# Pairing the value products of two key tiles in an interleaved attention kernel

## The chip, the cores and the metric

One core of one Trainium2 chip runs the kernel. The metric is the device time of one execution in microseconds, lower is better. Engines: TensorE (PE: matmuls; PEld: its weight loads), VectorE (DVE), ScalarE (ACT), GpSimd (POOL) and the DMA queues, which SyncE (SP) mostly issues.

## The reference

A pre-norm transformer layer in float32 on 2 sequences of 1024 tokens, width 512. The attention has 32 query heads of 16 and one key/value head for all of them, with ALiBi slopes and a causal mask:

```python
qkv = layernorm(x) @ Wqkv                      # 32 heads of q, one k, one v, each 16 wide
scores = einsum('bqhd,bkd->bhqk', q, k) * 16 ** -0.5 + alibi, causal
x = x + (softmax(scores) @ v) @ Wo
y = layernorm(x)
x = x + y @ W_base.T + b_base + lora_of_the_top_2_of_8_experts(y)
```

## The kernel before

The kernel has three stages: projections (to about 160 us of the profile), attention (to about 625 us), and the output projection with the feed-forward part. The change lies in the attention.

**Units and steps.** A unit is 4 heads of one sequence on 512 queries. Two units make a step's work: "early" (queries 0 to 511, 4 key tiles of 128) and "late" (queries 512 to 1023, 8 key tiles). So a unit pair has NTI = 12 tiles, numbered 0 to 11: 0 to 3 early, 4 to 11 late. A tile on the diagonal needs only part of the queries: tiles 0 to 3 are 512, 384, 256 and 128 queries wide, tiles 4 to 8 are 512 wide, and 9, 10, 11 are 384, 256 and 128 wide. There are NK = 16 unit pairs, and PE's step k (0 to 17) computes the row maxima of pair k among the scores and values of pair k - 1.

**Three kinds of PE work** are interleaved in a step; one instruction stream issues them in order.

- A *slot*, m0 to m41 (`max_slot`, line 561): bf16 matmuls into one of NSB = 3 PSUM banks (0 to 2). VectorE then takes the row maximum of it (line 972 for full slots, line 967 for diagonal ones). A slot waits until VectorE has freed the slot three before it (`slot_free`, line 543). Slots m0, m1, m17, m18 are 2 heads of 128 keys, m2, m3, m23, m24 are 2 heads of 256, m4 to m7 and m29 to m32 are 384 keys of one head, and the rest 512 keys of one head, but for m15 and m41: these transpose the finished maxima (line 550), for which VectorE must have finished the slots before them.
- A *score piece*, written S4.0, S4.1 and so on for tile and half (`scores`, lines 585 and 588): two heads at 2 banks, or all four heads for the narrow tiles 2, 3, 10 and 11, which have one piece. There are 2 score buffers, so a piece waits until ScalarE's exponential of the piece two before it has finished (`exp_done`, line 578). ScalarE (`exps`, line 791) writes the exponentials to `probs[:, n % 4]`, four tiles deep, and on diagonal tiles GpSimd zeroes the future (line 1152).
- A *value product*, V0 to V11 (`values_product`, line 606): for each of 4 heads a float32 matmul with a 128x32 weight into 32 of the 128 partitions of bank 7. Each matmul becomes two instructions, so a tile has 8. It waits for the tile's exponentials and its zeroing, and, at tiles 0 and 4, for ScalarE's copy of bank 7 (`copy_unit`, line 803) of the unit before.

`pe_order(k)` writes the order. Value products lag the scores by LAG = 2 tiles, so V10 and V11 of the pair before (marked ') fall into the next step. The slots are spread over the pieces by the columns of work done so far, each piece's own included, so that a large piece is preceded by many slots. For steps 2 to 15 it gives:

```
m0 S0.0 m1 m2 V10' m3 S0.1 m4 S1.0 V11' m5 S1.1 m6 m7 S2.0 m8 m9 V0 m10 S3.0 m11 m12 V1
m13 S4.0 m14 V2 m15 S4.1 m16 m17 S5.0 V3 m18 m19 S5.1 m20 S6.0 m21 m22 V4 m23 m24 S6.1 m25 S7.0
m26 m27 m28 V5 m29 S7.1 m30 S8.0 m31 m32 m33 V6 m34 S8.1 m35 S9.0 m36 m37 V7 m38 S9.1 m39 m40
S10.0 V8 S11.0 V9 m41
```

In step 16 there are no slots, and parts of the output projection (`out_proj`, line 630) stand ahead of some score pieces; step 17 is V10' V11' alone.

**ScalarE's order** is fixed too: exponentials in the order of the pieces, with `copy_unit` of the late unit before behind the first half of tile 1, and that of the early unit behind the first half of tile 5. SP stores the copied unit (`store_unit`) and moves the maxima (`max_rows`).

Of the kernel before, what the change touches and what calls it, by code (L numbers as in the profile page):

```python
# [40 lines left out]
CH = 512  # L41
QT = CH // P
NCH = B * S // CH
UH = 4
PAIRS = H // UH // 2
NB = 2 * PAIRS
NK = B * NB
# [12 lines left out]
LAG = 2  # L60
# [48 lines left out]
TILES = [(0, t, P * t) for t in range(QT)] + [(1, t, max(0, P * (t - QT))) for t in range(2 * QT)]  # L109
NTI = len(TILES)  # L110
DIAGS = 2 * QT

HALVES = [2 if CH - off > 256 else 1 for _, _, off in TILES]
# [4 lines left out]
def pe_order(k):  # L118


    work = []
    for n, (late, t, off) in enumerate(TILES):
        w = CH - off
        if 1 <= k <= NK:
            work.append((UH // HALVES[n] * w, ("scores", k - 1, (n, 0))))
        m, v = (k - 1, n - LAG) if n >= LAG else (k - 2, n - LAG + NTI)
        if 0 <= m < NK:
            work.append((UH * (CH - TILES[v][2]), ("values", m, v)))
        if 1 <= k <= NK and HALVES[n] == 2:
            work.append((UH // 2 * w, ("scores", k - 1, (n, 1))))  # L130
        if k == NK + 1 and n == LAG - 1:
            break
    slots = [("slot", k, r) for r in range(NSL)] if k < NK else []
    total = sum(w for w, _ in work)
    out, done, put = [], 0, 0
    for w, piece in work:
        done += w
        upto = min(NSL - 1, round(NSL * done / (SLOTS_BY * total)))
        out += slots[put:upto]
        put = max(put, upto)  # L140
        out.append(piece)
    return out + slots[put:]
# [25 lines left out]
def build(nc, x, wqkv, wo, wb, ag, lora, bias, ident_in, future_in, kmask_in, kalibi_in, qalibi_in, stair_in, iota_in, out):  # L168
    with ExitStack() as ctx:
        def sb(name, shape, dt=F32):  # L170
            return ctx.enter_context(nc.sbuf_tensor(name, shape, dt))
# [24 lines left out]
        work = sb("work", [P, 4 * UH * CH])  # L196
# [123 lines left out]
        def at_loop(base, i, per):  # L320

            return base if i is None else base + i * per
# [8 lines left out]
        def _(sp):  # L331
# [17 lines left out]
            def load_queries(c):  # L349


                sp.wait_ge(q_loaded, 16 * 6 * c)
                sp.wait_ge(q_stored, 16 * 4 * (c + 1))
                for n, (a, _) in enumerate(PARTS):
                    sp.dma_start(q_op_pairs[DH * n:DH * (n + 1), c % 2].rearrange("d g (h q) -> d (g h) q", q=CH),
                                 q_dram[c, a].rearrange("(h d) q -> d h q", d=DH)).then_inc(q_loaded, 16)

            def load_pair(g, i=None):


                sp.wait_ge(q_loaded, at_loop(16 * 12 * (1 + g), i, 16 * 12))
                plain_next()
                sp.wait_ge(s_full, at_loop(NSC * 2 * (g + 1), i, 2 * NSC))
                plain_next()
                gi = at_loop(g, i, 1)
                for late in range(2):
                    for n, (a, _) in enumerate(PARTS):
                        sp.dma_start(q_op_pairs[DH * n:DH * (n + 1), late, bass.ds(gi, 1)].rearrange("d g (h q) -> d (g h) q", q=CH),
                                     q_dram[NCH // 2 + late, a, bass.ds(gi * P, P)].rearrange("(h d) q -> d h q", d=DH)
                                     ).then_inc(q_loaded, 16)  # L370
# [121 lines left out]
        def _(pe):  # L492
# [36 lines left out]
            def values(c):  # L529

                bank = ring_bank(c, 5)
                pe.wait_ge(proj_free, 5 * c + 5)
                for t in range(QT):
                    last = nc.tensor.transpose(bank[:, 112 * t:112 * (t + 1)], kv[:, t * P:(t + 1) * P], ident[0:112, 0:112])
                last.then_inc(vt_full, 1)
# [74 lines left out]
            def step(k, i=None):  # L610
                for what, m, n in pe_order(k):
                    if k == 1 and what == "scores" and n == (0, 1):

                        values(NCH - 1)
                    if k == NK and what == "scores" and n in OUT_AMONG:
                        tile, g = divmod(OUT_AMONG.index(n), PAIRS)
                        out_proj(tile, None, (g,))
                    if k == NK and what == "scores" and n == (TURN_AT, 0):
                        turn_xn2(0, None)
                    {"slot": max_slot, "scores": scores, "values": values_product}[what](m, n, i)  # L620

            def out_proj(n, i, some=range(PAIRS)):
                if n == 0 and 0 in some:

                    pe.wait_ge(slot_free, NSL * NK)
                pe.wait_ge(att_ready, at_loop(n + 1, i, 2))
                if n >= 2:
                    pe.wait_ge(x1_ready, at_loop(n - 1, i, 2))
                for g in some:
                    last = nc.tensor.matmul(psum[:, n % 2], att[:, n % 2, g, :], wo_sb[:, g, :], start=(g == 0), stop=(g == PAIRS - 1))  # L630
                if g == PAIRS - 1:
                    last.then_inc(y_full, 1)

            def turn_xn2(n, i):
                pe.wait_ge(xn2_ready, at_loop(n + 1, i, 2))
                if n >= 2:
                    pe.wait_ge(xn2T_ready, at_loop(n - 1, i, 2))
                for k in range(KC):
                    last = nc.tensor.transpose(psum[:, 2 + n % 2, k * P:(k + 1) * P], xn2[:, n % 2, k * P:(k + 1) * P], ident[:])
                last.then_inc(turned2, 1)  # L640
# [52 lines left out]
            for b in range(B):  # L693
                if b:

                    pe.wait_ge(k_ready, NCH)
                    pe.wait_ge(q_loaded, 16 * 6 * 2 * PAIRS)
                    step(NB * b)
                step(NB * b + 1)
                if b:  # L700
                    pe.wait_ge(q_loaded, 16 * 6 * 2 * (1 + PAIRS))
                with pe.Fori(0, PAIRS - 1) as i:
                    step(NB * b + 2, i)
                    step(NB * b + 3, i)
# [17 lines left out]
        def _(act):  # L722
# [51 lines left out]
            def exps(m, n, i):  # L774
                w = CH - TILES[n][2]
                if NTI * m + n == 2:

                    act.wait_ge(q_stored, 16 * 4 * NCH)
                if NTI * m + n >= 4:

                    act.wait_ge(pv_done, at_loop(NTI * m + n - 3, i, 2 * NTI))
                heads = UH // HALVES[n]
                for hp in range(HALVES[n]):
                    idx = NSC * m + SC0[n] + hp
                    act.wait_ge(s_full, at_loop(idx + 1, i, 2 * NSC))
                    b0 = NSB + 2 * (idx % 2)
                    if heads == 2:
                        src = psum[:, b0:b0 + 2, 0:w]
                    else:
                        src = psum[:, b0:b0 + 2].rearrange("p b q -> p (b q)")[:, 0:UH * w].rearrange("p (j q) -> p j q", j=UH)  # L790
                    nc.scalar.activation(probs[:, n % 4, heads * hp:heads * (hp + 1), 0:w], src, ACT.Exp).then_inc(exp_done, 1)  # L791

                    if hp == 0 and n == LAG - 1 and m:
                        copy_unit(2 * m - 1, i)
                    if hp == 0 and n == QT + LAG - 1:
                        copy_unit(2 * m, i)

            def copy_unit(u, i=None):

                act.wait_ge(pv_done, at_loop(NTI * (u // 2) + (NTI if u % 2 else QT), i, 2 * NTI))  # L800
                if u >= 2:
                    act.wait_ge(o_stored, at_loop(32 * (u - 1), i, 128))
                nc.scalar.copy(o_sb[:, u % 2], psum[:, 7]).then_inc(o_copied, 1)

            def step(k, i=None):
                m = k - 1
                for n in range(NTI):
                    exps(m, n, i)
                    if k == NK and n == 5:
                        guess(0, None)  # L810
                    if k == NK and n == TURN_AT:
                        copy_xn2T(0, None)
                    if k == NK and n == NTI - 1:
                        guess(1, None)
# [467 lines left out]
```

## Time and profile before

| | before |
|---|---|
| runs | 787.32, 789.41, 790.63 us (median 789.41) |
| span of the profiled execution | 788.3 us |
| TensorE matmul busy | 691.0 us, 88% |
| VectorE busy | 576.1 us, 73% |
| ScalarE busy | 356.9 us, 45% |
| GpSimd busy | 187.6 us, 24% |
| mean granted TensorE clock | 0.956 |

The span runs from the first to the last instruction of one profiled execution; that execution's own time is known by its span alone, which lies inside the runs' spread. Busy time is a mean over stages with different limits, so the attention has to be read by itself. A matmul's modelled duration reaches past the start of the next, so start-to-start times tell what one costs.

### The profile page before, as it was taken

Reading aid. Unit: us, or ns where it says so; the run is one execution under the profiler, and the core shown is the slowest. Engines: PE = TensorE matmul, PEld = TensorE weight load, DVE = VectorE, ACT = ScalarE, POOL = GpSimd, SP = SyncE. Lnnn points to the kernel's source line nnn. Section 1 sums busy time; section 2 is a strip of 40 time slices with the busy share of each in tenths; the row PEclk is TensorE's granted clock in tenths of the full one; section 3 lists DMA queues with packets and bytes.
Section 4 is the critical chain, followed back from the end, with each engine's and each line's share of the span. In section 5 each row is a group of like instructions: output and inputs, shape, how many; then the busy total and the mean of one; then the engine's idle time right before and its main releaser. Section 6 shows DMA issues by size and latency. Waiting matters only on the chain.

```text
span 788.3 us, 16078 instructions
## 1 busy us (share of the span) xinstructions
PE 691.0 (88%) x4224; PEld 299.5 (38%) x4224; DVE 576.1 (73%) x1851; ACT 356.9 (45%) x493; POOL 187.6 (24%) x340
## 2 busy tenths in 40 slices
PE   4486535989999999999999999999999996699997
PEld 2243212333344344344334334334433453355553
DVE  6175344989988988989898998898892372366664
ACT  2133010246676666676666666666666410011111
POOL 0010101132242242133233224224233311222221
PEclk9888677999999999999999999999999999699999
DMA  9559799111043052062061085500000189400001
GB/s 235 71 150 128 113 129 224 67 37 64 31 59 55 29 70 43 27 74 52 16 96 39 16 108 91 84 30 16 15 29 30 37 141 162 117 27 27 27 27 53
DMA packets 37592, 56.06 MB, mean 71 GB/s; under 512 B 6028, under 2 KB 19468, under 8 KB 37524
## 3 DMA queue, kind: packets, MB, share of 16 engines
q1 hardware_dynamic: 35468, 49.17, 35.1%
q0 software_dynamic: 1792, 6.29, 2.4%
q8 instruction: 20, 0.33, 0.2%
q14 instruction: 24, 0.20, 0.1%
q10 hardware_dynamic: 288, 0.07, 0.0%
HBM read 35.72 MB, written 19.79 MB: 70 GB/s over the span
## 4 chain that ended last, share of the span: by engine, by line
PE 67%; DMA 14%; DVE 11%; issue 4%; SPq 3%; ACT 1%; DVEq 0%; POOL 0%; POOLq 0%; ACTq 0%
PE psum L606 19%; PE psum L561 16%; PE psum L588 9%; PE psum L630 5%; PE psum L652 5%; DMA q_dram<-work 4%; PE psum L585 4%; DMA arena<-q_dram 4%; DMA x_sb<-in_x 4%; DVE psum L967 3%; PE psum L522 3%; DMA out<-wqkv_sb 3%; DVE negm L972 2%; PE psum L647 1%; PE psum L662 1%
## 5 line engine op out<-in xcount | busy, mean ns | idle before, releaser
L791 ACT ACTIVATE work<-psum 128x1024 f32<-128x1024 f32 (+1 forms) x320 | 289.7, 943 | 161.6 <-PE psum L588 136.2
L967 DVE CUSTOM_DVE_ANT_0 psum<-psum,future 128x384 f32<-128x384 f32 (+3 forms) x512 | 240.0, 517 | 33.1 <-PE psum L561 26.2
L561 PE MATMUL psum<-k_op,arena 106*128 106x512 bf16 (+3 forms) x768 | 209.5, 331 | 35.6 <-DMA arena<-q_dram 20.2
L972 DVE TENSOR_REDUCE negm<-psum 128x1 f32<-128x512 f32 x256 | 163.1, 684 | 29.1 <-PE psum L561 28.4
L606 PE MATMUL psum<-work,v_op 128*32 128x512 f32 (+3 forms) x1536 | 164.3, 500 | 0.4 <-POOL work L1152 0.4
L588 PE MATMUL psum<-arena,k_op 109*128 (+4 forms) x640 | 158.6, 316 | 1.0 <-ACT work L791 0.8
L1152 POOL TENSOR_SCALAR_AFFINE_SELECT work<-work 128x512 f32<-128x512 f32 x128 | 81.6, 637 | 276.5 <-ACT work L791 276.5
L561 PEld LDWEIGHTS psum<-k_op,arena 106*128 (+1 forms) x768 | 69.9, 97 | 192.7 <-issue 95.7
L522 PE MATMUL psum<-work,wqkv_sb 128*128 128x512 f32 (+1 forms) x160 | 83.1, 642 | 15.9 <-issue 15.2
L585 PE MATMUL psum<-arena,k_op 116*128 (+1 forms) x512 | 85.1, 221 | 0.0
L588 PEld LDWEIGHTS psum<-arena,k_op 109*128 109x128 bf16 x640 | 60.3, 98 | 35.7 <-ACT work L791 8.9
L652 PE MATMUL psum<-wb_sb,x_sb 128*128 128x512 f32 x128 | 59.8, 611 | 14.5 <-DVE wqkv_sb L1076 14.5
L967 DVE DVE_READ_ACCUMULATOR2_ANT negm<- 128x1 f32 x512 | 72.1, 141 | 0.1
L630 PE MATMUL psum<-wo_sb,wqkv_sb 128*128 128x512 f32 x128 | 58.9, 595 | 0.5 <-issue 0.5
L585 PEld LDWEIGHTS psum<-arena,k_op 116*128 116x128 bf16 x512 | 45.9, 98 | 29.4 <-issue 16.1
L606 PEld LDWEIGHTS psum<-work,v_op 128*32 128x32 f32 x1536 | 30.4, 108 | 50.2 <-issue 39.4
L746 ACT ACTIVATE work<-psum 128x512 f32<-128x512 f32 x16 | 9.6, 598 | 87.0 <-PE psum L522 86.9
L1180 POOL TENSOR_TENSOR x_sb<-x_sb,bias_sb 128x512 f32<-128x512 f32 x16 | 20.3, 1266 | 117.6 <-DVE wqkv_sb L1076 117.6
L522 PEld LDWEIGHTS psum<-work,wqkv_sb 128*128 128x128 f32 (+1 forms) x160 | 31.1, 206 | 43.7 <-issue 42.9
L1116 POOL DMA_DIRECT2D q_dram<-work x16 | 12.5, 780 | 145.7 <-DVE work L912 80.0
L652 PEld LDWEIGHTS psum<-wb_sb,x_sb 128*128 128x128 f32 x128 | 23.9, 197 | 39.1 <-issue 24.3
L500 PE MATMUL psum<-ident,x_sb 128*128 128x128 f32 x64 | 10.9, 330 | 23.6 <-ACT work L736 13.2
(84 smaller groups left out, 453.1 us busy)
## 6 DMA issues: line engine op xcount, KB each, us to landing
o_dram<-o_sb SPq DMA_DIRECT2D x32, 256.0 KB
q_dram<-work POOLq DMA_DIRECT2D x16, 384.0 KB, 3.1
arena<-q_dram SPq DMA_DIRECT2D x12, 512.0 KB, 17.8
arena<-q_dram SPq DMA_DIRECT2D x48, 128.0 KB, 5.9
arena<-o_dram SPq DMA_DIRECT2D x32, 128.0 KB, 8.9
arena<-rcp_dram SPq DMA_DIRECT2D x32, 128.0 KB, 9.4
out<-wqkv_sb SPq DMA_DIRECT2D x16, 256.0 KB, 2.0
x_sb<-in_x SPq DMA_DIRECT2D x3, 1024.0 KB, 9.0
```

The source lines that it names most:

```text
L522: last = nc.tensor.matmul(bank[0:width], wqkv_sb[:, k, P * m:P * m + width], xnT[:, c % 2, k, :], start=(k == 0), stop=(k == KC - 1))
L561: last = nc.tensor.matmul(bank[:, a * width:(a + 1) * width], q_op[0:ROW_MAX, bass.ds(col, P)], k_op[0:ROW_MAX, b, k0:k0 + width], start=T ...
L585: last = nc.tensor.matmul(at[:, 0:P], k_op[0:STAIR_ROWS, b, t * P:(t + 1) * P], q_op[0:STAIR_ROWS, bass.ds(col, P)], start=True, stop=True)
L588: last = nc.tensor.matmul(at[:, diag:w], k_op[0:ROWS, b, t * P:(t + 1) * P], q_op[0:ROWS, bass.ds(col + diag, w - diag)], start=True, stop ...
L606: last = nc.tensor.matmul(psum[VW * j:VW * (j + 1), 7, off:CH], v_op[:, b * (S // P) + t, m % 2, :], probs[:, n % 4, j, 0:CH - off], start ...
L630: last = nc.tensor.matmul(psum[:, n % 2], att[:, n % 2, g, :], wo_sb[:, g, :], start=(g == 0), stop=(g == PAIRS - 1))
L652: nc.tensor.matmul(psum[:, 6 + n % 2], xn2T[:, n % 2, k, :], wb_sb[:, k, :], start=(k == 0), stop=False)
L791: nc.scalar.activation(probs[:, n % 4, heads * hp:heads * (hp + 1), 0:w], src, ACT.Exp).then_inc(exp_done, 1)
L967: last = nc.vector.tensor_tensor_reduce(keys, keys, future[:, CH - width:CH], -1.0, 3e38, ALU.add, ALU.min, negm[:, late, 0, j * QT + t:j ...
L972: nc.vector.tensor_reduce(dst, psum[:, idx % NSB, 0:len(js) * width].rearrange("p (a k) -> p a k", a=len(js)), AX_X, ALU.max, negate=True) ...
L1152: nc.gpsimd.affine_select(out=d, in_=d, compare_op=ALU.is_ge, fill=0.0, base=0, pattern=[[0, UH], [1, P]], channel_multiplier=-1).then_inc ...
L1180: nc.gpsimd.tensor_tensor(out=x1b[:, n % 2], in0=x1[:, n % 2], in1=bias_sb[:], op=ALU.add).then_inc(x1b_ready, 1)
```

## The change

`pe_order` places both pieces of a tile next to each other, and after every odd tile n one value entry that stands for the two tiles n - 3 and n - 2. `step` then issues the two value products one after the other, with no slot or score piece between them. ScalarE's two `copy_unit` calls move from behind the first half of their tile to behind the second.

```diff
@@ pe_order
         if 1 <= k <= NK:
-            work.append((UH // HALVES[n] * w, ("scores", k - 1, (n, 0))))
-        m, v = (k - 1, n - LAG) if n >= LAG else (k - 2, n - LAG + NTI)
-        if 0 <= m < NK:
-            work.append((UH * (CH - TILES[v][2]), ("values", m, v)))
-        if 1 <= k <= NK and HALVES[n] == 2:
-            work.append((UH // 2 * w, ("scores", k - 1, (n, 1))))
+            work += [(UH // HALVES[n] * w, ("scores", k - 1, (n, hp))) for hp in range(HALVES[n])]
+        if n % 2:
+            m, v = (k - 1, n - 1 - LAG) if n > LAG else (k - 2, n - 1 - LAG + NTI)
+            if 0 <= m < NK:
+                work.append((UH * (2 * CH - TILES[v][2] - TILES[v + 1][2]), ("values", m, v)))
@@ tensor engine, step
                     {"slot": max_slot, "scores": scores, "values": values_product}[what](m, n, i)
+                    if what == "values":
+                        values_product(m, n + 1, i)
@@ scalar engine, exps
-                    if hp == 0 and n == LAG - 1 and m:
+                    if hp == 1 and n == LAG - 1 and m:
                         copy_unit(2 * m - 1, i)
-                    if hp == 0 and n == QT + LAG - 1:
+                    if hp == 1 and n == QT + LAG - 1:
                         copy_unit(2 * m, i)
```

For steps 2 to 15 the order becomes (a block of two value products in brackets):

```
m0 S0.0 m1 m2 S0.1 S1.0 m3 S1.1 m4 m5 [V10+11]' m6 m7 S2.0 S3.0 m8 m9 m10 m11 m12 [V0+1]
m13 S4.0 m14 S4.1 m15 S5.0 m16 m17 S5.1 m18 m19 [V2+3] m20 S6.0 m21 S6.1 m22 S7.0 m23 m24 S7.1
m25 m26 m27 m28 m29 [V4+5] m30 S8.0 m31 S8.1 m32 S9.0 m33 S9.1 m34 m35 m36 m37 m38 [V6+7]
m39 m40 S10.0 S11.0 [V8+9] m41
```

## Rows read from the trace of the kernel before

**Rows 1.** The page: the span, and the busy time of three engines

```profile
span 788.3 us, 16078 instructions
...
PE 691.0 (88%) x4224; PEld 299.5 (38%) x4224; DVE 576.1 (73%) x1851; ACT 356.9 (45%) x493; POOL 187.6 (24%) x340
```

**Rows 2.** Windows: stretch, length, busy time by engine, granted clock, DMA

```profile
207.00:580.00 373.00, 363.92 (x2839) 146.67 (x2842) 336.87 (x1082) 244.21 (x287) 110.42 (x235) 1.00 0.30 50
```

**Rows 3.** TensorE's timeline (start, length, instructions): V4 of steps 1 and 15

```profile
178.12 1.07 PE L606 MATMUL psum<-work,v_op 128*32 128x512 f32 x8
...
579.93 1.07 PE L606 MATMUL psum<-work,v_op 128*32 128x512 f32 x8
```

**Rows 4.** Chain of waits, 399 to 428 us: shares; V5, V7, V9, V11'

```profile
by line: PE psum L606 35.7%; PE psum L561 30.9%; PE psum L588 18.5%; PE psum L585 7.3%; DVE psum L967 4.8%; DVE negm L972 1.9%; PE psum L550 1.4%; DVE negm L967 0.8%; issue 0.3%
...
411.07 1.00 PE psum L606 x8
...
416.80 1.00 PE psum L606 x8
...
420.68 0.78 PE psum L606 x8
...
424.59 0.36 PE psum L606 x8
```

**Rows 5.** TensorE's timeline, 406 to 411 us: m21 m22 V4, then m25 to m28

```profile
406.49 0.59 PE L561 MATMUL psum<-k_op,arena 106*128 106x512 bf16 x2
407.01 1.06 PE L606 MATMUL psum<-work,v_op 128*32 128x512 f32 x8
408.01 0.61 PE L561 MATMUL psum<-k_op,arena 106*128 106x256 bf16 x4
...
408.89 0.38 PE L561 MATMUL psum<-k_op,arena 106*128 106x512 bf16 x1
409.11 0.59 PE L588 MATMUL psum<-arena,k_op 109*128 109x512 bf16 x2
409.55 0.38 PE L561 MATMUL psum<-k_op,arena 106*128 106x512 bf16 x1
410.14 0.39 PE L561 MATMUL psum<-k_op,arena 106*128 106x512 bf16 x1 [0.21 <-DVE negm L967]
410.68 0.39 PE L561 MATMUL psum<-k_op,arena 106*128 106x512 bf16 x1 [0.15 <-DVE negm L972]
```

**Rows 6.** TensorE's timeline at the end of attention: S11.0, then V9 and V10'

```profile
622.21 0.39 PE L585 MATMUL psum<-arena,k_op 116*128 116x128 bf16 x4
622.53 1.28 PE L606 MATMUL psum<-work,v_op 128*32 128x384 f32 x16
```

**Rows 7.** Timeline of two engines: a copy, exponentials, and S0.1 to S1.1

```profile
405.87 0.59 ACT L803 COPY o_sb<-psum 128x512 f32<-128x512 f32 x1
...
409.09 1.94 ACT L791 ACTIVATE work<-psum 128x1024 f32<-128x1024 f32 x2 [0.78 <-PE psum L588]
...
423.48 0.22 PE L585 MATMUL psum<-arena,k_op 116*128 x1
...
424.12 1.73 ACT L791 ACTIVATE work<-psum 128x1024 f32<-128x1024 f32 x2 [0.83 <-PE psum L588]
...
425.20 0.23 PE L585 MATMUL psum<-arena,k_op 116*128 x1
```

**Rows 8.** VectorE's timeline: full slots, a 384-wide one, and m41

```profile
409.94 2.48 DVE L972 TENSOR_REDUCE negm<-psum 128x1 f32<-128x512 f32 x4
...
414.07 0.60 DVE L967 CUSTOM_DVE_ANT_0 psum<-psum,future 128x384 f32<-128x384 f32 x1
...
414.58 2.77 DVE L972 TENSOR_REDUCE negm<-psum 128x1 f32<-128x512 f32 x4
...
421.71 0.28 DVE L956 COPY m_t<-psum 16x128 f32<-16x128 f32 x1 [1.29 <-PE psum L550]
```

## The prediction

> **What bounds the kernel now.** I read the page first [rows 1]: TensorE is busy 88% of 788.3 us, VectorE 73%. Then the windows of the steady attention [rows 2]: in 373 us TensorE is busy 363.9 (98%, clock 1.00) and VectorE 336.9 (90%). So TensorE is the bound there, with VectorE close behind. V4 of step 1 starts at 178.12 and V4 of step 15 at 579.93 [rows 3]: 14 periods of 28.70 us. In a period VectorE is busy 28.70 x 0.90 = 25.9 us, so it could go at most 2.8 us faster. The chain of waits over one period [rows 4] is 93% TensorE, 36% of it value products, and only 7% VectorE.
>
> **What a fused block saves.** In the chain [rows 4] a value block costs 1.00 us for 512 queries, 0.78 for 384 and 0.36 for 128: (1.00 - 0.36) / 3 = 0.213 per 128 queries and 0.147 that doesn't depend on the width. There is a piece on the way in too: m21 and m22 start at 406.49 and stream 0.22 each (408.89 to 409.11), so are through at 406.93, and V4 starts at 407.01 [rows 5]: 0.09. A block so pays 0.237 for its edges. The trace has one fused pair already, V9 and V10' in step 17 [rows 6]: 1.28 long, 1.21 without the 0.07 by which modelled ends overrun, for 640 queries x 0.213 / 128 = 1.07 of streaming. Its edges inside are 0.147 once, not twice. So each fusion saves 0.237; six in a period save 1.42 us.
>
> The Trainium skill (TensorEngine Tiling, Key Properties) says that changing the tiling mode, and not merely the tile, drains TensorE. The trace agrees, with the 0.09 and the 0.147; by that rule alone the change gains, which is the second rival below.
>
> **What it adds: the order.** Nothing is added in instructions; TensorE's own work is the same but for the 1.42. By the rows it is, in a period of the new order: slots 8.3 us (0.22 for each 512-wide or 2x256-wide one, 0.165 for 384, 0.11 for 2x128, 0.2 for m15 and m41), score pieces 8.0 (0.44 for two heads of 512, 0.33 for 384, 0.46 and 0.23 for the single ones), blocks 9.1 (1.94 for 512+512, 1.73 for 512+384, 0.88 for 256+128, edges included). Sum 25.3. Before, the same sum is 26.75, and the period 28.70, so 1.95 are waits.
>
> Two loops with shallow buffers now matter, both read from rows.
>
> *Scores and exponentials.* S0.1 starts at 423.48, its exponential at 424.12, and S1.1, two pieces on, at 425.20 [rows 7]: 1.72 us from a piece to the second after it. Two exponentials back to back take 1.94, one about 1.03, so the next comes 0.91 later. Before, a block stood between every two pieces at most; now four stand in a row. With the first at 0, the third can't start before 1.72, nor the fourth before 2.63. TensorE's own work puts the fourth at 1.8 to 2.1 with the slots between.
>
> *Slots and VectorE.* A full slot takes VectorE 2.48 / 4 = 0.62, a 384-wide one 0.51 (414.07 to 414.58) [rows 8]. A slot issued is ready for VectorE 0.41 later (0.39 for the matmul, 0.35 for a 384-wide one). VectorE turns to the next at 409.94, and the freed bank lets m27 start at 410.14 [rows 5, 8]: 0.20 after a diagonal slot; m28 starts 410.68, 0.12 after the full one's 0.62. The new order puts five slots ahead of [V0+1], [V4+5] and [V6+7] and then nothing for VectorE in the block. Take D, when VectorE is done with the third slot before the last. The last slot starts at D + 0.12, the block at D + 0.12 + 0.22 + 0.09, it ends 1.85 later at D + 2.28, and the next slot is ready at D + 2.69. VectorE has three slots from D, 1.86 us: idle 0.8. With 8-instruction blocks that end came 0.85 sooner, and VectorE didn't idle.
>
> The two loops aren't cover for each other. While TensorE waits for an exponential, it issues no slots, so VectorE runs dry; then the five slots in a row wait for VectorE.
>
> **The walk.** I followed the new order by hand with these numbers, clock at 0 where m41 starts. From the end of [V4+5] to the end of [V6+7], counted from the former: m30 0, ready 0.35, VectorE to 0.87. S8.0 0.16. m31 0.60, S8.1 0.77, m32 1.21. S9.0 would start at 1.37 and waits for S8.0's exponential: 1.86. m33 2.19, ready 2.60, VectorE having waited 0.5. S9.1 waits to 2.78. m34 3.11, m35, m36. m37 needs m34's bank: 4.38; m38 needs m35's: 4.88. Block 5.19 to 7.04. Before, V5 to V7 end to end took 416.80 - 411.07 = 5.73 [rows 4]. So 1.3 us are lost in this part alone.
>
> The whole period walked so, ends of blocks: [V10+11]' 4.40, [V0+1] 9.27, [V2+3] 13.88, [V4+5] 21.64, [V6+7] 28.68, [V8+9] 31.54. TensorE's waits in it:
>
> - for exponentials 2.8: S1.0 0.49, S1.1 0.38, S5.0 0.48, S5.1 0.15, S7.0 0.38, S7.1 0.04, S9.0 0.49, S9.1 0.37
> - for slots 3.5: m10 to m12 1.0, m19 0.1, m26 to m29 1.5, m37 and m38 0.9
>
> 25.3 + 6.3 = 31.6, against 28.70. The waits I can name before come to 1.4 of the 1.95 (m27 and m28 0.7 [rows 5], S1.1 0.16 [rows 7], and some 0.5 at m2, m6 and m8 in the same timeline), so 0.5 per period is in neither walk; it may or may not be there after. I take between +2.9 and +3.4: +3.1.
>
> m41 itself costs VectorE 1.29 idle now [rows 8]; it comes 2.86 after [V6+7], with m39 and m40 to chew on for 1.7, which is 1.2 to 1.3 again. No change.
>
> **The copies.** `copy_unit` takes ScalarE 0.59 [rows 7]. Behind S1.1's exponential it finds V11' done at about the same time (both near 4.3 on the walk's clock), and then S2.0's exponential is behind it; that is wanted by S4.0, 4 us later. The other ends at 14.6, before S6.0's exponential is due (14.7). Cost nothing; without that cover 0.59 per copy, on the third piece of the next four. The stores on SP's queue wait for the copies and start about 1 us later; behind each stands the transfer of the maxima, which the late scores need at S4.0 only, 9.5 after m41 in the walk. GpSimd zeroes tiles over 2 us ahead of their block. The DMA share is 0.30 [rows 2], with more time to hide in.
>
> The Trainium skill (Perfetto Trace Analysis, Optimization Strategy) advises interleaving stretches that different engines limit. No row here shows such a rewrite; it speaks against a change that takes interleaving out, on the side of the walk.
>
> **The sum.** Steps 1 to 15: 15 x 3.1 = 46.5. Step 16 has no slots: its four pieces in a row wait 1.3 us twice, less four fusions and what it waits now: about +1. Step 17 was fused already. 46.5 + 1 = 47.5. The profiled execution would go from 788.3 to 835.8; the median of the runs lies 1.1 above it, so 837. About 0.5% (4 us) is what a measurement of this kernel can tell from no change.
>
> **Rivals.**
>
> 1. *Forecast: both loops bite*, 820 to 862: 0.70.
> 2. *Only the edges count.* The place is TensorE's queue: if the waits stay at 1.95 per period, it gains 15 x 1.42 + 1 = 22 us: 767. For it: TensorE is 93% of the chain, and VectorE has 2.8 to spare. Against it: the 1.72 and the 0.62 are measured, and the buffers are 2 and 3. It decides as soon as the new waits are under 1.95 + 1.42 = 3.4 of the 6.3 walked. 0.08, with anything from 762 to 785.
> 3. *Only the exponentials bite*, VectorE catches up out of its 2.8: 2.8 - 1.42 = +1.4 per period, 15 x 1.4 = 21: 810 (800 to 820). The bursts of slots speak against it. 0.13.
> 4. *The waits lower the clock.* It is 1.00 now at 98% busy. At half clock for a tenth of TensorE's 25.3 us, each period gains 2.5: 837 + 38 = 875. The longest single wait walked is 0.5 us, which speaks against it. 0.05.
> 5. *The gain and the waits cancel*, 785 to 793: 0.04.
>
> The range leaves out 2, 5, 4 and a part of 3's low end: 804 to 862. Faster 0.08, within 0.5% 0.03, slower 0.89.
>
> **What would show it.** Value blocks of sixteen, 1.85 us start to next start at 512+512. V4 to V4 31.6 to 32.1 us. TensorE busy share of the attention down from 98% to about 82%, VectorE from 90% to about 80%. Waits of the second halves (S5.0, S7.0, S9.0) on ScalarE near 0.4 to 0.5 each, waits of slots on VectorE ahead of the blocks, and VectorE idle 0.7 to 0.8 after each 512-wide block. If V4 to V4 is under 28.7, the loops don't bind and the walk is wrong; if slots wait but pieces don't, the 1.72 is.

## The result: 7.6% slower

The changed kernel takes 849.24 us (median of 4 runs, 848.54 to 849.95), the kernel before 789.15 (787.32 to 790.63). The ratio is 1.0761, with a 95% interval of 1.0741 to 1.0781. The forecast was 837 in a range of 804 to 862, slower with a chance of 0.89.

The page of the changed kernel, span and busy times, answers to [rows 1]:

```profile
span 847.7 us, 16078 instructions
...
PE 703.9 (83%) x4224; PEld 311.0 (37%) x4224; DVE 579.7 (68%) x1851; ACT 353.4 (42%) x493; POOL 186.9 (22%) x340
```

The instructions are the same in number, and every engine has a smaller share of a longer span. The same stretch by windows, to be held against [rows 2] (start and end, length, busy PE, PEld, DVE, ACT, POOL, clock, DMA share, GB/s):

```profile
207.00:580.00 373.00, 331.08 (x2482) 136.87 (x2480) 300.29 (x950) 213.87 (x253) 93.62 (x203) 1.00 0.28 48
```

TensorE is busy 89% where it was 98%, VectorE 81% where it was 90%, and the granted clock is still 1.00, the 2.4 GHz level. Both engines that were nearly full now have time to spare. (The busy share of TensorE runs to the matmuls' modelled ends, so short waits hide in it: it reads 89%, where the forecast had 82%.) TensorE's timeline, the block that begins with V4 in step 1 and in step 15 [rows 3]:

```profile
184.82 1.92 PE L605 MATMUL psum<-work,v_op 128*32 128x512 f32 x16
...
641.30 1.92 PE L605 MATMUL psum<-work,v_op 128*32 128x512 f32 x16
```

14 periods of 32.61 us, against 28.70 before (forecast: 31.6 to 32.1): 54.7 us of the 59.4 by which the span grew. The first of these blocks starts 6.7 us later than V4 did, and from the last to the end it takes 2.0 us less (206.4 against 208.4). The 6.7 is mostly its later place in the order: in step 9 V4 starts 13.35 us after m41 of step 8 in the kernel before and 20.04 now.

The chain of waits over a period, by line, answers to [rows 4]:

```profile
by line: PE psum L605 29.2%; ACT work L792 18.1%; PE psum L560 13.8%; PE psum L587 12.3%; DVE psum L968 11.1%; DVE negm L973 7.4%; PE psum L584 3.8%; issue 2.0%; DVE negm L968 1.5%; PE psum L549 1.3%; ACTq L786 0.2%
```

Before, TensorE's lines made up 94% of the chain (the prediction has 93%). Now the exponentials (line 792) hold 18% and VectorE 20% of it.

The stretch that the prediction walked, on TensorE's timeline in step 9: S6.0, S6.1, S7.0, S7.1 with their slots, m25 to m29, the block, m30 ([rows 5] show the old one):

```profile
439.17 0.60 PE L587 MATMUL psum<-arena,k_op 109*128 109x512 bf16 x2
...
439.83 0.60 PE L587 MATMUL psum<-arena,k_op 109*128 109x512 bf16 x2
440.26 0.38 PE L560 MATMUL psum<-k_op,arena 106*128 106x512 bf16 x1
440.95 0.61 PE L587 MATMUL psum<-arena,k_op 109*128 109x512 bf16 x2 [0.31 <-ACT work L792]
...
442.30 0.83 PE L560 MATMUL psum<-k_op,arena 106*128 106x512 bf16 x2
443.50 0.39 PE L560 MATMUL psum<-k_op,arena 106*128 106x512 bf16 x1 [0.38 <-DVE negm L968]
444.05 0.39 PE L560 MATMUL psum<-k_op,arena 106*128 106x512 bf16 x1 [0.16 <-DVE negm L973]
444.65 0.34 PE L560 MATMUL psum<-k_op,arena 106*128 106x384 bf16 x1 [0.21 <-DVE negm L973]
444.91 1.92 PE L605 MATMUL psum<-work,v_op 128*32 128x512 f32 x16
446.77 0.34 PE L560 MATMUL psum<-k_op,arena 106*128 106x384 bf16 x1
...
451.76 0.39 PE L560 MATMUL psum<-k_op,arena 106*128 106x512 bf16 x1 [0.21 <-DVE negm L973]
452.08 1.92 PE L605 MATMUL psum<-work,v_op 128*32 128x512 f32 x16
453.93 0.60 PE L560 MATMUL psum<-k_op,arena 106*128 106x512 bf16 x2
```

S7.0 starts 1.78 us after S6.0 and is marked as waiting for ScalarE, and the last three slots ahead of the block wait for VectorE. The block takes 1.86 us from its start to the next one. From block end to block end it is 453.93 - 446.77 = 7.16 (walked: 7.04; before: 5.73). VectorE's timeline around the block:

```profile
443.31 2.48 DVE L973 TENSOR_REDUCE negm<-psum 128x1 f32<-128x512 f32 x4
445.70 0.56 DVE L968 CUSTOM_DVE_ANT_0 psum<-psum,future 128x384 f32<-128x384 f32 x1
446.18 0.14 DVE L968 DVE_READ_ACCUMULATOR2_ANT negm<- 128x1 f32 x1
447.14 0.57 DVE L968 CUSTOM_DVE_ANT_0 psum<-psum,future 128x384 f32<-128x384 f32 x1 [0.83 <-PE psum L560]
```

The three slots ahead of the block are done at 446.3, the next is ready at 447.1: idle 0.83 (the prediction's queue: 2.69 - 1.86 = 0.83). Behind [V0+1] and [V6+7] of the same step VectorE's idle time is 0.61 and 0.75 (until 434.66 and 454.36).

### The profile page after: what moved, and what is told of

It is laid out like the page before. It is cut to its first block, busy times and chain, and to the rows that moved or that the text cites. A ratio compares the mean times of both kernels' runs of the same rounds, so it can differ in the third digit from the quotient of the medians.

```text
span 847.7 us, 16078 instructions
## 1 busy us (share of the span) xinstructions
PE 703.9 (83%) x4224; PEld 311.0 (37%) x4224; DVE 579.7 (68%) x1851; ACT 353.4 (42%) x493; POOL 186.9 (22%) x340
## 4 chain that ended last, share of the span: by engine, by line
PE 55%; DVE 14%; DMA 14%; ACT 8%; issue 5%; SPq 3%; DVEq 0%; ACTq 0%; POOLq 0%
PE psum L605 16%; PE psum L560 11%; PE psum L587 8%; ACT work L792 8%; PE psum L631 5%; PE psum L653 5%; DVE negm L973 5%; DMA q_dram<-work 4%; DVE psum L968 4%; DMA arena<-q_dram 3%; PE psum L584 3%; DMA x_sb<-in_x 3%; DMA out<-wqkv_sb 3%; PE psum L521 2%; DVE negm L968 1%
## 5 line engine op out<-in xcount | busy, mean ns | idle before, releaser
L792 ACT ACTIVATE work<-psum 128x1024 f32<-128x1024 f32 (+1 forms) x320 | 278.8, 940 | 211.5 <-PE psum L587 210.1
L560 PE MATMUL psum<-k_op,arena 106*128 106x512 bf16 (+3 forms) x768 | 214.9, 333 | 58.9 <-DMA arena<-q_dram 21.6
L973 DVE TENSOR_REDUCE negm<-psum 128x1 f32<-128x512 f32 x256 | 167.2, 687 | 56.1 <-PE psum L560 54.4
L560 PEld LDWEIGHTS psum<-k_op,arena 106*128 (+1 forms) x768 | 71.7, 97 | 203.3 <-issue 92.1
L605 PE MATMUL psum<-work,v_op 128*32 128x512 f32 (+3 forms) x1536 | 145.1, 496 | 0.0
L584 PE MATMUL psum<-arena,k_op 116*128 (+1 forms) x512 | 82.5, 221 | 12.6 <-ACT work L792 11.3
L587 PEld LDWEIGHTS psum<-arena,k_op 109*128 109x128 bf16 x640 | 57.2, 98 | 55.7 <-ACT work L792 29.5
L605 PEld LDWEIGHTS psum<-work,v_op 128*32 128x32 f32 x1536 | 40.4, 109 | 63.5 <-issue 50.0
L521 PEld LDWEIGHTS psum<-work,wqkv_sb 128*128 128x128 f32 (+1 forms) x160 | 30.8, 204 | 44.5 <-issue 43.7
L631 PEld LDWEIGHTS psum<-wo_sb,wqkv_sb 128*128 128x128 f32 x128 | 22.7, 190 | 21.8 <-issue 21.8
```

The lines of the kernel that those rows point to most:

```text
L521: last = nc.tensor.matmul(bank[0:width], wqkv_sb[:, k, P * m:P * m + width], xnT[:, c % 2, k, :], start=(k == 0), stop=(k == KC - 1))
L560: last = nc.tensor.matmul(bank[:, a * width:(a + 1) * width], q_op[0:ROW_MAX, bass.ds(col, P)], k_op[0:ROW_MAX, b, k0:k0 + width], start=T ...
L584: last = nc.tensor.matmul(at[:, 0:P], k_op[0:STAIR_ROWS, b, t * P:(t + 1) * P], q_op[0:STAIR_ROWS, bass.ds(col, P)], start=True, stop=True)
L587: last = nc.tensor.matmul(at[:, diag:w], k_op[0:ROWS, b, t * P:(t + 1) * P], q_op[0:ROWS, bass.ds(col + diag, w - diag)], start=True, stop ...
L605: last = nc.tensor.matmul(psum[VW * j:VW * (j + 1), 7, off:CH], v_op[:, b * (S // P) + t, m % 2, :], probs[:, n % 4, j, 0:CH - off], start ...
L973: nc.vector.tensor_reduce(dst, psum[:, idx % NSB, 0:len(js) * width].rearrange("p (a k) -> p a k", a=len(js)), AX_X, ALU.max, negate=True) ...
```

## The experiments

Most verdicts rest on the *straight period*, from m41 of step 8 to m41 of step 9: in TensorE's program these two steps are written out, while steps 2 to 7 and 10 to 15 stand in loops. It is read from two rows of TensorE's timeline, here of the kernel before:

```profile
393.66 0.28 PE L550 MATMUL psum<-ident,negm 128*16 128x128 f32 x1
...
421.40 0.28 PE L550 MATMUL psum<-ident,negm 128*16 128x128 f32 x1
```

and of the changed kernel:

```profile
424.87 0.28 PE L549 MATMUL psum<-ident,negm 128*16 128x128 f32 x1
...
456.80 0.28 PE L549 MATMUL psum<-ident,negm 128*16 128x128 f32 x1
```

| kernel | median us | ratio to before | straight period | periods in loops |
|---|---|---|---|---|
| before | 789.15 | | 27.74 | 28.5, 29.0 |
| changed | 849.24 | 1.076 | 31.93 | 32.4, 33.0 |
| a_short_exp | 812.91 | 1.030 | 29.13 | 30.2, 30.8 |
| a_short_max | 790.10 | 1.000 | 28.60 | 29.1 |
| a_short_both | 752.74 | 0.954 | 25.51 | 26.4 |
| b_short_both | 755.86 | 0.958 | 26.70 | 26.8, 27.1 |
| copies_only | 798.12 | 1.0115 | 28.48 | 29.0, 29.5 |
| pieces_paired | 781.79 | 0.9912 | 27.36 | 28.0, 28.3 |
| slot_inside | 831.90 | 1.0545 | 30.13 | 31.5, 32.1 |
| narrow_fused | 795.25 | 1.0069 | 28.33 | 29.0, 29.6 |
| a_copies_back | 872.50 | 1.1047 | 33.25 | 34.0, 34.5 |
| one_wide | 807.22 | 1.0218 | 28.84 | 29.5, 29.9 |
| slots_regrouped | 831.46 | 1.0520 | 31.01 | 31.3, 31.7 |
| paired_89 | 779.13 | 0.9860 | 27.11 | 27.8, 28.3 |

Loops run two steps at a time, hence two values where they differ; steps 10 to 12, some of which fall outside, are left out. Times of whole kernels are medians of 2 runs for a_short_exp, a_short_both and b_short_both, of 8 for a_short_max and of 4 for the others. The first four experiments ran with the kernel before at 789.71, the next four at 788.73, the last four at 789.91.

**a_short_exp: the exponentials cut.**

```diff
-                    nc.scalar.activation(probs[..., 0:w], src, ACT.Exp)
+                    e = 64 if m else w
+                    nc.scalar.activation(probs[..., 0:e], src[:, :, 0:e], ACT.Exp)
```

It leaves out the exponentials of all but the first 64 queries, so its output is of no use; it serves the timing alone, as do the next three kernels.

> The changed kernel, but each exponential from unit pair 1 on covers only the first 64 queries of a head (the rest of the tile is left as it was), so ScalarE takes about 0.25 us where it took 0.6 to 1.03. All else, the order and TensorE's own work, stays. Theory A (both loops cost): the waits of the third and fourth score piece go (2.8 us a period of the walk), those for slots stay and take a little back: 849 to 805-820 us. Theory B (VectorE's bursts alone set the pace, the exponential waits only fill time that slots would wait for anyway): 840 to 850. Theory C (the exponentials alone cost): back to or below 790.

Measured: 812.91. The straight period falls by 31.93 - 29.13 = 2.80; the walk charged 2.8 to exponentials. That they agree so closely is partly luck: single waits are off by about 0.1 (S7.0: 0.38 walked, and 440.95 - 440.26 - 0.22 = 0.47 in the rows above). Theories B and C are both out by more than 20 us.

**a_short_max: the maxima cut.**

```diff
-  keys = psum[:, idx % NSB, a * width:(a + 1) * width]
-  last = nc.vector.tensor_tensor_reduce(keys, keys, future[:, CH - width:CH], ...
+  keys = psum[:, idx % NSB, a * width:a * width + 64]
+  last = nc.vector.tensor_tensor_reduce(keys, keys, future[:, CH - width:CH - width + 64], ...
-  nc.vector.tensor_reduce(dst, psum[...].rearrange("p (a k) -> p a k", a=len(js)), ...
+  nc.vector.tensor_reduce(dst, psum[...].rearrange("p (a k) -> p a k", a=len(js))[:, :, 0:64], ...
-  nc.scalar.activation(probs[...], src, ACT.Exp)
+  nc.scalar.activation(probs[...], src, ACT.Exp, scale=0.01)
```

The scale keeps the exponentials finite and leaves their length as it was: one of 1024 columns takes 1.026 us in both kernels.

> The changed kernel, but VectorE reduces only the first 64 keys of each slot, so a slot takes it about 0.25 us and not 0.5 to 0.65; the exponentials get a scale of 0.01 so that they stay finite, at the same length. Theory A: the waits for slots (3.5 us a period) go, those for exponentials (2.8) stay: 849 to about 796 (790-805). Theory C (the exponentials alone cost): 840 to 850. Theory B (bursts alone): under 790.

Measured: 790.10, at the low edge of theory A. The period falls by 3.33 (walked for slots: 3.5).

**a_short_both and b_short_both: both cuts, on the changed kernel and on the one before.** They leave out what the two above leave out, and have the scale of 0.01.

> The changed kernel with both cuts: exponentials of 64 queries and maxima over 64 keys. Neither loop can hold TensorE up, so the period is its own work in the new order, 25.3 us, plus 0.5 to 1.1 that the walk left out: about 26.1, so V4 to V4 26 to 26.5 and 745 to 755 us in all.

> The kernel before with both cuts: the price of the edges by itself. If a fused block saves 0.237 us at its edges, six a period, this one's period is 1.42 us longer than the changed kernel's with the same cuts, 27.3 to 27.8, and the whole some 21 us longer, about 767. If the edges cost nothing, the two are the same within 4 us.

Measured: 752.74 as expected, and 755.86 where 767 was expected. The two cuts give 36.3 and 59.1 us singly, 95.4 in sum, and 96.5 together: the two kinds of wait hardly overlap. The edges by themselves (the costs at both ends of a value block, which a fusion saves), on the straight period (rows of a_short_both, then of b_short_both):

```profile
369.93 0.28 PE L549 MATMUL psum<-ident,negm 128*16 128x128 f32 x1
...
395.44 0.28 PE L549 MATMUL psum<-ident,negm 128*16 128x128 f32 x1
```

```profile
372.58 0.28 PE L550 MATMUL psum<-ident,negm 128*16 128x128 f32 x1
...
399.28 0.28 PE L550 MATMUL psum<-ident,negm 128*16 128x128 f32 x1
```

25.51 and 26.70: six fusions save 1.19, 0.20 each, where I had 0.237. But in the loops' periods the difference is only about 0.45 (26.4 against 26.8 and 27.1), so some 60% of the saving is lost in loops. One period of a_short_both, from m15 of step 11 (431.69) to m15 of step 12 (463.59), takes 31.9. That single wait hides a part of the gain in the whole times, 752.74 against 755.86. In the waits from 207 to 560 us, weight loads of slots stand on "issue", that is on nothing that another engine releases, for 55.2 us in a_short_both and for 36.6 us in b_short_both (same stretch, about the same work):

```profile
PEld psum L560 <- issue: 55.2, 124, 0.9
```

```profile
PEld psum L561 <- issue: 36.6, 71, 1.5
```

In loops the addresses of slots and pieces are computed in registers. That a longer row of them without a value block between outruns what TensorE's sequencer can issue fits this, but no run took the registers away: it is argued, not shown. For the long period, the chain of waits of a_short_both from 415 to 450 us has one large piece, a transfer that ends at 450.8:

```profile
438.94 11.85 DMA m_dram<-m_part
```

so there the transfer of the maxima came late for the scores; TensorE waits 4.0 us for it.

**copies_only: the copies of bank 7 alone.**

```diff
-                    if hp == 0 and n == LAG - 1 and m:
+                    if hp == 1 and n == LAG - 1 and m:
...
-                    if hp == 0 and n == QT + LAG - 1:
+                    if hp == 1 and n == QT + LAG - 1:
```

> The kernel before, with the two copies of bank 7 moved behind the second half of their tile, and the order of TensorE untouched. Prediction's view: the copies are covered, so within 4 us of before. Rival: each copy pushes back the exponentials behind it by 0.59 us and TensorE waits for that: two per period, 15 periods, up to +18 us.

Measured: 798.12, ratio 1.0115 (1.0090 to 1.0139), 9.4 us more than before. The prediction's view is out, and the time lies inside the rival's "up to +18", but its mechanism is another: TensorE waits for the copy itself. The copy behind S5.1's exponential, then V4 on TensorE, and the sum of such waits from 207 to 580 us, a line that the kernel before doesn't have:

```profile
410.38 0.58 ACT L803 COPY o_sb<-psum 128x512 f32<-128x512 f32 x1
...
411.02 1.07 PE L606 MATMUL psum<-work,v_op 128*32 128x512 f32 x8 [0.50 <-ACT o_sb L803]
...
PE psum L606 <- ACT o_sb L803: 5.5, 13, 0.5
```

In the old order the copy behind S5.1's exponential comes so late that V4, the late unit's first product into bank 7, waits 0.5 for it. There are 13 such waits for 26 copies: V0, behind the other copy, doesn't wait (the next expectation names V0, which is wrong).

**a_copies_back: the same two lines, undone on the changed kernel.**

> The changed kernel with the two copies of bank 7 put back behind the first half of their tile. The copies moved alone in the old order cost 9 us, since V0 waited for them. In the new order the products that a copy waits for come only after both halves, so behind the first half ScalarE would stand still before the second half's exponential. If the move belongs with the new order, this is slower than 849, by the wait of an exponential for a copy, 0.6 to 1.5 us a period: 858 to 870. If the move cost 9 us here as well, it is 840.

Measured: 872.50, 2.5 above the expected range, the period 1.32 longer. In the new order the products that a copy waits for come behind both halves, so a copy behind the first half holds up the second half's exponential. ScalarE's waits for those products from 207 to 580 us, in this run and in the changed kernel:

```profile
ACT o_sb L804 <- PE psum L605: 27.2, 22, 1.8
...
ACT o_sb L804 <- PE psum L605: 8.8, 22, 0.9
```

In the changed kernel no line has TensorE waiting for a copy, and the exponential behind a copy waits for its own piece (here S6.0's, on ScalarE's timeline):

```profile
439.08 0.59 ACT L804 COPY o_sb<-psum 128x512 f32<-128x512 f32 x1 [0.16 <-PE psum L605]
439.87 3.77 ACT L792 ACTIVATE work<-psum 128x1024 f32<-128x1024 f32 x4 [0.20 <-PE psum L587]
```

So in the new order the moved copies cost nothing that these rows show, as the prediction said, and in the old order they do.

**pieces_paired: halves side by side, one product per tile, copies moved.**

```diff
         if 1 <= k <= NK:
-            work.append((UH // HALVES[n] * w, ("scores", k - 1, (n, 0))))
+            work += [(UH // HALVES[n] * w, ("scores", k - 1, (n, hp))) for hp in range(HALVES[n])]
         m, v = (k - 1, n - LAG) if n >= LAG else (k - 2, n - LAG + NTI)
...
-        if 1 <= k <= NK and HALVES[n] == 2:
-            work.append((UH // 2 * w, ("scores", k - 1, (n, 1))))
```

This is against the kernel before; the copies' two lines are those of copies_only. The order is then `m20 S6.0 m21 S6.1 m22 m23 m24 V4 m25 S7.0 m26 S7.1 m27 m28 m29 V5`.

> Both halves of a tile next to each other, as in the changed kernel, and the copies moved, but a single value product after every tile, so two score pieces in a row and not four, and three slots in a row and not five. If the cost lies in four pieces and five slots in a row, this is back near before: 785 to 796 us. If the pairing of halves costs by itself, 800 or more. The edges are as before (26.7 us of own work in a straight period).

Measured: 781.79, ratio 0.9912 (0.9888 to 0.9936): faster than expected and than before. From 207 to 580 us TensorE's slots wait less for VectorE's diagonal work, first before and then here:

```profile
PE psum L561 <- DVE negm L967: 5.6, 14, 1.2
...
PE psum L559 <- DVE negm L965: 1.1, 1, 1.1
```

The pairing of halves doesn't cost; what the changed kernel has beyond it, the missing block between two tiles and the slots that gather ahead of the wide one, does.

**slot_inside: a slot between the two products of the wide blocks** (`m25 m26 m27 V4 m28 V5 m29`).

```diff
-        out += slots[put:upto]
+        if slots and piece[0] == "values" and piece[2] in (0, 4, 6) and upto - put >= 3:
+            out += slots[put:upto - 2] + [piece] + [slots[upto - 2], ("values", piece[1], piece[2] + 1), slots[upto - 1]]
...
```

> The changed kernel, but in [V0+1], [V4+5] and [V6+7] one of the five slots stands between the two products and one behind them; the score pieces stay four in a row. It pays 0.24 of edges for each of three blocks, and VectorE has a slot to do in the middle: by the prediction's queue each block releases the next slot 0.48 us sooner, three a period, so 849 to about 829 (824-840). If VectorE's idle time after the blocks weren't on the path, it would be 849 or, with the edges, 860.

Measured: 831.90. The straight period falls by 1.80, the ones in loops by 0.9; expected were 1.4. So VectorE's idle time behind the blocks, together with the row of slots ahead of them, was on the path; the edit breaks up both and doesn't part them.

**slots_regrouped: the slots moved into the waits for exponentials** (`m20 S6.0 S6.1 m21 m22 m23 m24 S7.0 m25 m26 S7.1 m27 m28 m29 V4 V5`).

```diff
+        if len(pieces) == 4 and len(some) >= 6:
+            counts = {6: (1, 0, 2, 1, 2), 7: (1, 0, 3, 1, 2), 8: (1, 0, 3, 1, 3), 9: (1, 0, 3, 2, 3), 10: (1, 0, 4, 2, 3), 11: (1, 0, 4, 2, 4)}[len(some)]
+            part, put = [], 0
+            for c, p in zip(counts, pieces + [order[end - 1]]):
+                part += some[put:put + c] + [p]
+                put += c
```

(`counts` holds the slots ahead of each of the four pieces and of the block.)

> The changed kernel's pieces and blocks, but its slots placed so that they fill the waits for exponentials: none between the first two of four pieces, two to four ahead of the third, and at most three ahead of a block. The waits on ScalarE (2.8 us a period) go for the most part; VectorE still has nothing behind each wide block (0.8, three times). By theory A: 849 to 815-832. If the two waits had simply been added, -2.8 a period, 807; if VectorE alone sets the pace, no change.

Measured: 831.46, the period 0.92 shorter. From 207 to 580 us TensorE waits for exponentials for 8.6 and 7.4 us at the pieces' two lines in the changed kernel, and for 1.7 and 2.7 us here, but VectorE goes on waiting for slots (line 988 is the diagonal ones'). Here:

```profile
DVE psum L988 <- PE psum L580: 32.9, 56, 0.9
...
PE psum L607 <- ACT work L812: 2.7, 14, 0.2
PE psum L604 <- ACT work L812: 1.7, 7, 0.4
```

The changed kernel:

```profile
DVE psum L968 <- PE psum L560: 31.2, 52, 0.9
...
PE psum L584 <- ACT work L792: 8.6, 27, 0.5
PE psum L587 <- ACT work L792: 7.4, 24, 0.4
```

So with the exponentials mostly covered the block still starves VectorE (its idle time at this line stays, 32.9 against 31.2), and a third of the 2.8 comes back.

**narrow_fused: three fusions that leave VectorE enough, in the old order.** V3 is issued behind V2, V11' behind V10', and V8 ahead of V9.

```diff
-        if 0 <= m < NK:
+        if 0 <= m < NK and v not in (3, 11) and v != 8:
...
+            if v in (2, 10):
+                work.append((UH * (CH - TILES[v + 1][2]), ("values", m, v + 1)))
+            if v == 9:
+                work.insert(-1, (UH * CH, ("values", m, 8)))
```

> The order of before, with three fusions only: V2 with V3, V10' with V11', and V8 with V9 (S11.0 ahead of both). The first two blocks are 0.88 us long, VectorE's three slots outlast them, and nowhere more than two score pieces follow each other without a block. It saves three edges, 0.6 to 0.7 us a period, 9 to 10 us in all: 789 to about 780. Rival: in steps inside loops the saving is lost in issuing (the kernels with both cuts differ by 1.2 us in a straight period and by only 0.45 in a loop's), then 784 to 787.

Measured: 795.25, ratio 1.0069 (1.0047 to 1.0091): a miss of 15 us, and the expectation's sentence that nowhere more than two score pieces follow each other without a block was false. With V3 gone from between them, S4.1, S5.0, S5.1 and S6.0 follow each other, and so do S0.1, S1.0, S1.1 and S2.0. The waits from 207 to 580 us have two lines that the kernel before doesn't have:

```profile
PE psum L590 <- ACT work L796: 5.7, 13, 0.4
...
PE psum L593 <- ACT work L796: 2.8, 12, 0.2
```

VectorE's waits for slots stay short here, none longer than 0.4 us (in the changed kernel up to 0.9), though [V8+9] is a wide block. So the run shows the loop of the exponentials nearly by itself: three saved edges don't pay for two runs of four pieces.

**one_wide: a single wide block, [V4+5], in the order of pieces_paired.**

```diff
-        if 0 <= m < NK:
+        if 0 <= m < NK and v != 4:
+            if v == 5:
+                work.append((UH * (CH - TILES[v - 1][2]), ("values", m, v - 1)))
             work.append((UH * (CH - TILES[v][2]), ("values", m, v)))
```

The order around the block is `m20 S6.0 m21 S6.1 m22 S7.0 m23 m24 S7.1 m25 m26 [V4+5] m27 m28 m29 m30 S8.0`: two slots ahead of the block and four behind, where the changed kernel has five and one.

> The order of pieces_paired (782 us) with one fused wide block, [V4+5], and so one run of four wide score pieces per period. Saved: one edge, 0.24. Cost by the walk: 0.4 of exponential waits at S7.0 and S7.1, and 0.7 to 0.8 of VectorE standing idle behind the block: net +0.9 a period, 782 to about 795 (789-800). If fusing as such gains and only the sum of all fusions overloads ScalarE and VectorE, it is 778 to 782.

Measured: 807.22. The sign is right and the size is not: one wide block costs 1.48 a straight period (28.84 against 27.36), not 0.9. S7.0 and ScalarE:

```profile
444.85 0.60 PE L589 MATMUL psum<-arena,k_op 109*128 x2 [0.58 <-ACT work L792]
```

```profile
443.27 0.59 ACT L804 COPY o_sb<-psum 128x512 f32<-128x512 f32 x1
443.74 2.89 ACT L792 ACTIVATE work<-psum 128x1024 f32<-128x1024 f32 x3
```

S6.0 starts at 442.69, and its exponential could at 443.3, but V3's copy is in the way until 443.74. S7.0 starts at 444.85, 2.16 behind S6.0 and not 1.72. Here the copy's cover was gone, at the place that the prediction named for it. VectorE idles behind this block too:

```profile
449.33 1.29 DVE L973 TENSOR_REDUCE negm<-psum 128x1 f32<-128x512 f32 x2 [0.84 <-PE psum L562]
```

The copy's 0.44 accounts for most of the 0.6 by which the cost exceeds the walk's; the rest isn't parted.

**paired_89: one fusion where nothing is in its way**, S10.0 S11.0 [V8+9] m41, in the order of pieces_paired (the diff is one_wide's with 8 and 9 for 4 and 5).

> The order of pieces_paired with one fusion where no run of wide pieces and no starving of VectorE comes with it: S10.0 S11.0 [V8+9], ahead of m41, which leaves sooner too. It saves 0.24 us a period: 782 to 778 (776-781). If an edge is lost in issue or VectorE's turn, 782.

Measured: 779.13, ratio 0.9860 (0.9837 to 0.9884). The straight period is 0.25 shorter than that of pieces_paired: there the edges of one fusion come back in full. In loops it is 27.8 against 28.0 for one of the two periods and the same for the other, and the whole is 2.7 us less (3.8 when each is held against its own measurement of before), where 15 x 0.24 = 3.6 were expected. It is the fastest kernel of the study that leaves nothing out, 1.4% below before.

## Why the prediction was right, and what was 12 us off

**What bounds the kernel.** Right, with the warning that mattered: TensorE was the bound with 2% to spare, VectorE with 10%, and ScalarE, at 65% in that stretch, was named nowhere as a bound. It became one through the distance of two pieces, not through its load.

**The edges.** 0.237 per fusion and 1.42 per period were predicted; 1.19 was measured in straight periods, 0.25 for the single one in paired_89, and about 0.45 for all six in loops' periods. (By the rows the way in costs 407.01 - 406.93 = 0.08, not 0.09.) The drain that the Trainium skill names (TensorEngine Tiling, Key Properties) fits a cost at each edge, but no run parts it from whatever else happens there. Rival 2 (only the edges count) is out: the saving is real, but the waits rose by 6.42 - 1.04 = 5.4 a period. With both loops cut out, the changed kernel is faster by 3.1 us, 0.4%, its one long wait for a transfer included, and not by the 22 us of rival 2.

**The order.** The walk's block ends against the trace, in us from m41 (456.80 - 424.87 = 31.93 for the last):

| | [V10+11]' | [V0+1] | [V2+3] | [V4+5] | [V6+7] | [V8+9] |
|---|---|---|---|---|---|---|
| walked | 4.40 | 9.27 | 13.88 | 21.64 | 28.68 | 31.54 |
| measured | 4.49 | 9.36 | 14.08 | 21.90 | 29.06 | 31.93 |

The waits were walked at 2.8 and 3.5, 6.3 in sum. The cut kernels show 2.80 and 3.33 singly and 31.93 - 25.51 = 6.42 together. The walk is 0.39 short. Two prices in it are low, and their shares weren't parted: from a piece to the second after it the step shows 1.77, 1.78 and 1.79 (S4.0, S6.0 and S8.0) where the walk has 1.72, and a diagonal slot of 512 keys takes VectorE 0.65 (431.42 to 432.07), for which the prediction has no price of its own. TensorE's own work was added up a little wrong: 8.3 + 8.0 + 9.1 is 25.4 and not 25.3; 25.51 was measured. Rival 3 (only the exponentials) is out by a_short_max, rival 5 (cancelled) by the time itself, rival 4 by the clock of 1.00.

**The step that was off** is the sum's "+3.1". The walk describes a straight period, 31.54, and I held it against 28.70, the mean over steps that mostly stand in loops; the 1.95 of "waits" before that came of it I could name only to 1.4, and took back half of the rest. The trace has both kinds of period. Straight, the kernel before takes 27.74, so its waits are 27.74 - 26.70 = 1.04. Straight, the change so parts into -1.19 + 6.42 - 1.04 = +4.19; all three are read from the same four periods, so that they add up to 31.93 - 27.74 is no test of them. The walk against the straight period before would have given 31.54 - 27.74 = +3.8. In loops both kernels take 0.5 to 1.3 more than straight, which nearly cancels: 32.7 - 28.8 = 3.9. No term of the prediction stood for that, so it was luck that it cancels. 14 periods x (3.91 - 3.1) = 11.3 us is what the forecast lacked in 837 against 849.

**The copies.** Right in the new order, by a_copies_back and by waits of TensorE that name no copy. Without cover a copy of 0.59 on ScalarE cost TensorE 0.5 at V4 in copies_only and about 0.45 at S7.0 in one_wide.

**m41.** No change was forecast, and its wait on VectorE's timeline is 1.14 at 457.12 (before: 1.29; forecast: 1.2 to 1.3). In the changed kernel's waits from 207 to 580 us the copy of the maxima waits 7.8 and 4.6 us for slots and transposes, against 11.4 and 5.2 before.

**Step 16** was put at +1. No run tests it by itself, but m41, which keeps its place at the end of a step, shows it. In step 1 it starts at 192.95 before and at 196.72 now, 3.8 later, so step 1 costs what the others do. From its start in step 15 (594.69 and 653.20) to the end it is 193.6 and 194.5: +0.9 for step 16 and all behind it.

## What to carry to other kernels

Where one in-order engine feeds several others through a few banks, count for each consumer how much work the banks hold (here 3 x 0.62 = 1.86 us for VectorE), and keep every stretch that doesn't feed it shorter than that. Count too how long one trip takes (1.72 us for two score buffers), and put other work between the pieces to fill it. A saving on the feeding engine is worth what it saves only while that holds: here six fusions saved 1.2 us a period and brought 5.4 us of waits more (6.4 for 1.0). Before a walk is held against a period, pick a period of the same kind; and price a lone fusion at the place where the consumers have nothing to lose, since there it paid in full in the straight period.

## What the runs showed of the hardware that I had not expected

- Periods in loops are longer than the same periods written out, in every kernel of the study: 28.5 and 29.0 against 27.74 before, 32.4 and 33.0 against 31.93 after, and, with hardly a wait for other engines left, 26.4 against 25.51 in a_short_both. In b_short_both it is only 26.8 and 27.1 against 26.70. What it hangs on stays open.
- Waits of TensorE for two different engines add up. The prediction said that the two loops aren't cover for each other; that they would add up so exactly, 36.3 and 59.1 us singly and 96.5 together, it did not.
